# Selective scan in one kernel: GpSimd multiplies a whole step in one instruction, and products and C rows have two places each

## The chip, the cores and the metric

One Trainium2 chip, one of its cores. The metric is the device time of one execution in microseconds. Most repeated executions of a kernel agree within 0.3%.

## The reference, cut to what matters

The kernel computes two layers. The first is attention-like and a mixture of experts, and the change does not touch it. The second is a Mamba block over 4 batches of 2048 tokens, followed by a small mixture of experts on 512 tokens. The part that the change touches is the selective scan, with 512 channels (d) and 16 states (n):

```python
def step(h, ins):
    u_t, dt_t, B_t, C_t = ins
    dA = jnp.exp(dt_t[:, :, None] * A)
    h = dA * h + (dt_t * u_t)[:, :, None] * B_t[:, None, :]
    y_t = jnp.einsum('bdn,bn->bd', h, C_t)
    return (h, y_t)
...
y = y + x_conv * D
y = y * jax.nn.silu(z)
return y @ W_out
```

## The kernel before

Everything is f32. Five engines run their own instruction lists, written out by hand, and meet at counting semaphores (`wait_ge`, `then_inc`); an engine that waits holds everything that stands behind the wait in its list.

For each batch, `projection` makes u, dt, dt*u and the rows of B and C; `selective_scan` runs the recurrence; `output` does the gate, the output product and two layer norms. The first `projection` stands alone, then a loop of three runs scan, output and the next projection in one block, and the last block runs scan and output.

The scan of a batch has 64 steps: 4 quarters (`q`) of 512 tokens (CHUNK), and in each the 16 states (`n`). Channels lie on partitions in 4 groups of 128 (`m`, KI is 4). Step s works like this:

- ScalarE (`scalar`): `decay` makes exp(dt*A) for all four groups, 2048 columns, in `da[s % 2]` (L1600). `save` copies the last column of h to `state` in the first three quarters (L1606). `times_b` multiplies the turned dt*u by B in four instructions (L1593). Once a quarter `keep_y` copies the finished y out of PSUM (L1611), after the last gather of the quarter before; it stands ahead of the `decay` of the quarter's third step.
- TensorE (`tensor`): four `to_channels` of four transposes each bring B*dt*u back to channels in PSUM, one for each group (L1528; called the fills below). Two `gather` of eight transposing matmuls each add the products of h and C into the y banks, for groups 0 and 1 and for groups 2 and 3 (L1547), and the second also adds one skip term (L1553). Its list is: fill of step s+1 for groups 0 and 1, first gather of step s-1, fill of step s+1 for groups 2 and 3, second gather of step s-1. After the last step, `z_proj` of the output stage (L1694) stands behind the gathers of step 62, and the gathers of step 63 stand behind it.
- VectorE (`vector`): four scans of 512 columns (L1655), one for each group, each from `da` and a PSUM bank, into `h[s % 2]`. In the quarters after the first they start from `state`.
- GpSimd (`gpsimd`): two products of 1024 columns, `h` times the C row (L1639), for groups 0 and 1 and for groups 2 and 3. They go round three places: two in `hc` and one in `kept`, a tile that holds the 512 tokens for the last mixture of experts once the scan is over.
- The sync queue (`sync`): the C row of a step comes from DRAM, broadcast to 128 partitions, into one of three places of `c_sb` (L1576), when the product that read that place is done.

h has two places. So the first scan of step s waits for the first product of step s-2, and the third scan for the second product; `hr` counts products, `sd` scans, `yr` gathers.

Of the kernel before, what the change touches and what calls it, by code (L numbers as in the profile page):

```python
# [10 lines left out]
ALU = mybir.AluOpType  # L11
# [3 lines left out]
P = 128  # L15
BATCH, SEQ, D = 4, 2048, 256
TILES = SEQ // P
CHUNK = 512
# [8 lines left out]
KI = INNER // P  # L27
# [986 lines left out]

def layer1(nc, t, out, top, tile, sem, sems, clear, bank, ident, ones, layer_norm, x2_dram, x2T_dram, bc_dram):
    with ExitStack() as L:
        kept = tile(L, "kept", [P, MOE_TOK // P, D])
        with ExitStack() as W:
            w_z = tile(W, "w_z", [P, KC, INNER])
            shared = tile(W, "shared", [P, KI, CHUNK])  # L1020
# [44 lines left out]
            with ExitStack() as s:  # L1065
# [3 lines left out]
                b_cols = tile(s, "b_cols", [P, TILES, STATE])  # L1069
                da = tile(s, "da", [P, 2, KI, CHUNK])  # L1070
                h = tile(s, "h", [P, 2, KI, CHUNK])
                hc = tile(s, "hc", [P, 2, 2, CHUNK])
                c_sb = tile(s, "c_sb", [P, 3, CHUNK])
                state = tile(s, "state", [P, STATE, KI])
                halo = tile(s, "halo", [P, KI, TAPS - 1])
                outside = set(sems)

                def project(g, xT_ready, xT_parts, before=None):
                    return projection(nc, tile, sem, bank, ident, xT, w_x_in, w_dt, w_x, cw, cb, bdt, a_neg, bc_dram, u, dt,
                                      dtu, b_cols, turned0, tok, da, h, hc, c_sb, halo, xT_ready, xT_parts, before)  # L1080

                def scan(g):
                    return selective_scan(nc, sem, bank, ident, tok, u, dt, dtu, b_cols, turned0, skip, a_neg, bc_dram,
                                          kept, da, h, hc, c_sb, state)

                def finish(g, b, ahead, scanned):
                    return output(nc, b, ahead, g, tile, sem, bank, ident, tok, xT, w_z, w_x_in, w_out, t["W_in"], t["W_out"],
# [102 lines left out]


def projection(nc, tile, sem, bank, ident, xT, w_x_in, w_dt, w_x, cw, cb, bdt, a_neg, bc_dram, u, dt, dtu, b_cols,
               turned0, tok, da, h, hc, c_sb, halo, xT_ready, xT_parts, before=None):

    WIDE = TAPS - 1 + HALF
    xin = h[:, :, :, :].rearrange("p a m n -> p (a m n)")[:, 0:3 * WIDE].rearrange("p (w n) -> p w n", w=3)
    slots = da[:, :, :, :].rearrange("p a m n -> p (a m n)")
    xc = slots[:, 0:3 * HALF].rearrange("p (w n) -> p w n", w=3)
    bc = slots[0:2 * STATE, 3 * HALF:4 * HALF]
    th = hc[:, :, :, :].rearrange("p a m n -> p a (m n)")  # L1200
    pr, cp, cv, tr, uu, z = (sem(n) for n in (
        "in_proj", "in_copied", "conv_done", "tanh_ready", "u_ready", "pad_zeroed"))
    bcr, bcc, bt, bk, dr, mn, ln, du, dd, ct = (sem(n) for n in (
# [10 lines left out]
    class Steps:  # L1214
        @staticmethod
        def sync(sp):
            for half in range(2):
                sp.wait_ge(bcc, half + 1)
                sp.dma_start(bc_dram[:, half * HALF:(half + 1) * HALF], bc[:, :]).then_inc(ct, 16)
                if half == 0:  # L1220
                    sp.wait_ge(ct, 16)
                    for n in range(3):
                        sp.dma_start(c_sb[:, n, :], bc_dram[STATE + n, 0:CHUNK].partition_broadcast(P)).then_inc(cl, 16)

        @staticmethod
        def stored(sp):
            sp.wait_ge(ct, 2 * 16)
            sp.wait_ge(cl, 3 * 16)
            if before is not None:
                before.stored(sp)  # L1230

# [233 lines left out]
    return Steps  # L1465


def selective_scan(nc, sem, bank, ident, tok, u, dt, dtu, b_cols, turned0, skip, a_neg, bc_dram, kept, da, h, hc, c_sb,
                   state):

    def turned(q):
# [2 lines left out]
    QUARTERS, N = CHUNKS, STATE  # L1474

    bt_at = [tok[:, 8 * w:8 * w + 8, :].rearrange("p (c i) d -> p c (i d)", c=4) for w in range(2)]
    hc_at = [hc[:, 0, :, :], hc[:, 1, :, :], kept[:, :, :].rearrange("p (m i) d -> p m (i d)", m=2)]

    steps = [(q, n) for q in range(QUARTERS) for n in range(N)]
    S = len(steps)  # L1480

# [1 line left out]
    for s_, (q, n) in enumerate(steps):  # L1483
# [6 lines left out]
    xt, xd, pd, br, dr, sd, sv, hr, yr, yd = (sem(n) for n in (  # L1490
        "dtu_turned", "dtu_kept", "b_times_dtu", "b_ready", "decay_ready", "scan_done", "state_saved", "product",
        "y_added", "y_kept"))
    cl = [sem(f"c_loaded{w}") for w in range(3)]

    def span(q):
        return slice(q * CHUNK, (q + 1) * CHUNK)
# [3 lines left out]

    class Steps:
        all_scanned, y_kept, b_turned = (sd, KI * S), (yd, 4 * QUARTERS), (br, KI * (S - 1))
        y_kept_half, products = (yd, 4 * QUARTERS - 2), (hr, 2 * S)
        @staticmethod
        def tensor(pe, after):
            def place(x):
                kind, i, j = fills[number[x] - 4]
                if kind == "b":
                    pe.wait_ge(sd, KI * i + j + 1)
                else:  # L1510
                    pe.wait_ge(xd, 4 * (i - 1) + j + 1)

            def turn(q, c):
                x = ("turn", q, c)
                place(x)
                for m in range(KI):
                    at = q * CHUNK + c * P
                    op = pe.transpose(fill_bank(x)[:, m * P:(m + 1) * P], dtu[:, m, at:at + P], ident[:, :])
                op.then_inc(xt, 1)

            def to_channels(s_, m):
                x = ("b", s_, m)
                place(x)
                if m == 0:
                    if s_ >= 2:
                        pe.wait_ge(pd, 4 * (s_ - 1))
                for c in range(4):
                    op = pe.transpose(fill_bank(x)[:, c * P:(c + 1) * P], bt_at[s_ % 2][:, c, m * P:(m + 1) * P],  # L1528
                                      ident[:, :])
                op.then_inc(br, 1)  # L1530

            def fill(x):
                kind, i, j = x
                if kind == "b":
                    to_channels(i, j)
                else:
                    turn(i, j)

            def gather(s_, j):
                q, n = steps[s_]  # L1540
                if n == 0 and j == 0 and q:
                    pe.wait_ge(yd, 4 * q)
                pe.wait_ge(hr, 2 * s_ + j + 1)
                for i in range(2):
                    m = 2 * j + i
                    for c in range(4):
                        op = pe.matmul(bank(Y + c)[:, m * P:(m + 1) * P], hc_at[(2 * s_ + j) % 3][:, i, c * P:(c + 1) * P],  # L1547
                                       ident[:, :], start=(n == 0 and m == 0), stop=(n == N - 1),
                                       is_transpose=True, skip_group_check=True)
                if j == 1:  # L1550
                    c, m = n // 4, n % 4
                    at = q * CHUNK + c * P
                    op = pe.matmul(bank(Y + c)[:, m * P:(m + 1) * P], u[:, m, at:at + P], skip[:, m, :],  # L1553
                                   start=False, stop=(n == N - 1), skip_group_check=True)
                op.then_inc(yr, 1)

            done = number["b", 1, 0]
            for s_ in range(S):
                for m in range(KI):
                    while s_ + 1 < S and done <= number["b", s_ + 1, m]:  # L1560
                        fill(fills[done])
                        done += 1
                    if s_ and m % 2:
                        gather(s_ - 1, m // 2)
            after.z_proj(pe, 0)
            gather(S - 1, 0)
            gather(S - 1, 1)
            after.z_proj(pe, 1)

        @staticmethod  # L1570
        def sync(sp):
            for s_, (q, n) in enumerate(steps):
                if s_ < 3:
                    continue
                sp.wait_ge(hr, 2 * (s_ - 3) + 2)
                sp.dma_start(c_sb[:, s_ % 3, :], bc_dram[N + n, span(q)].partition_broadcast(P))\  # L1576
                  .then_inc(cl[s_ % 3], 16)

        @staticmethod
        def scalar(act, after):  # L1580
# [48 lines left out]
        @staticmethod  # L1629
        def gpsimd(pool):  # L1630
            for s_ in range(S):
                if s_ >= 3:
                    pool.wait_ge(cl[s_ % 3], 16 * (s_ // 3))
                for j in range(2):
                    p = 2 * s_ + j
                    pool.wait_ge(sd, KI * s_ + 2 * j + 2)
                    if p >= 3:
                        pool.wait_ge(yr, p - 2)
                    pool.tensor_tensor(hc_at[p % 3], h[:, s_ % 2, 2 * j:2 * j + 2, :],  # L1639
                                       c_sb[:, s_ % 3, :].unsqueeze(1).broadcast_to([P, 2, CHUNK]), ALU.mult)\  # L1640
                        .then_inc(hr, 1)

        @staticmethod
        def vector(dve):
            for s_, (q, n) in enumerate(steps):
                for m in range(KI):
                    if s_:
                        dve.wait_ge(dr, s_)
                        dve.wait_ge(br, KI * (s_ - 1) + m + 1)
                    if m % 2 == 0 and s_ >= 2:  # L1650
                        dve.wait_ge(hr, 2 * (s_ - 2) + m // 2 + 1)
                    if m == 0 and 2 <= s_:
                        dve.wait_ge(sv, min(s_ - 1, (QUARTERS - 1) * N))
                    first = state[:, n, m:m + 1] if q else 0.0
                    dve.tensor_tensor_scan(h[:, s_ % 2, m, :], da[:, s_ % 2, m, :],  # L1655
                                           fill_bank(("b", s_, m)), first, ALU.mult, ALU.add).then_inc(sd, 1)
# [375 lines left out]
```

## Time and profile before

| | us |
|---|---|
| median of 3 runs | 3993.24 |
| lowest and highest run | 3987.85, 3995.3 |
| the profiled execution | 3995.58 |
| its span, first to last instruction | 3993.8 |
| VectorE busy in the span | 2801.4 (70%) |
| GpSimd busy in the span | 1510.7 (38%) |
| mean granted TensorE clock, of full speed | 0.95 |

The span is the profiled execution from its first to its last instruction; 1.8 us of its time lie outside. Times of rows below count from the span's start. A timeline row gives start, length, engine (PE is the matmuls, PEld the weight loads, DVE VectorE, ACT ScalarE, POOL GpSimd), line, operation, output and inputs, count, and in brackets the idle time before it and what ended it. Rows of several instructions in a row are merged: their length runs from the first start to the last end.

### The profile page before, as it was taken

How to read it: one execution, taken by the hardware profiler on the slowest of the kernel's cores; microseconds unless marked ns; L12 is line 12 of the kernel's file. 1: busy time of each engine (PE TensorE's matmuls, PEld its weight loads, DVE VectorE, ACT ScalarE, POOL GpSimd, SP SyncE). 2: the span in 40 equal slices, each digit the busy share in tenths (PEclk: the TensorE clock that was granted, in tenths of full speed). 3: DMA queues.
4: the chain of work that ended last, by engine and by line, in shares of the span. 5: the costliest groups of instructions: out<-in, count | busy, mean ns of one | idle time of the engine just before them, and what ended most of it. 6: DMA issues, size and time to landing. Idle time of an engine off the chain costs nothing. (4 is left out here: it accounts for less than half of the span.)

```text
span 3993.8 us, 53655 instructions
## 1 busy us (share of the span) xinstructions
PE 3410.1 (85%) x19632; PEld 2572.8 (64%) x19632; DVE 2801.4 (70%) x4919; ACT 1955.7 (49%) x3164; POOL 1510.7 (38%) x757
## 2 busy tenths in 40 slices
PE   5898889897999889878888978889888898888879
PEld 2686748783778558663678635777348774488744
DVE  4676457653766467645799766997759987599855
ACT  3222232222223322224799346995459963599700
POOL 1100410031102210030699404995039960199800
PEclk9899989998999989989999999999999999899989
DMA  3000100001000100020111200112101121011220
GB/s 142 1 1 22 65 1 1 22 22 43 1 22 1 64 1 1 22 86 10 36 56 56 74 25 28 57 56 72 36 18 57 56 77 41 10 58 56 68 85 6
DMA packets 103168, 155.31 MB, mean 39 GB/s; under 512 B 15698, under 2 KB 54482, under 8 KB 101346
## 3 DMA queue, kind: packets, MB, share of 16 engines
q1 hardware_dynamic: 102882, 151.62, 11.7%
q8 instruction: 166, 2.72, 0.3%
q14 instruction: 120, 0.98, 0.1%
HBM read 124.81 MB, written 26.78 MB: 38 GB/s over the span
## 5 line engine op out<-in xcount | busy, mean ns | idle before, releaser
L1639 POOL TENSOR_TENSOR hc<-h,c_sb 128x1024 f32<-128x1024 f32 x344 | 810.9, 2382 | 539.7 <-DVE h L1655 532.0
L1655 DVE TENSOR_TENSOR_SCAN h<-da,state,PS 128x512 f32<-128x512 f32 x768 | 902.2, 1257 | 18.2 <-PE PS L1528 12.9
L1528 PE MATMUL PS<-ident,tok 128*128 128x128 f32 x4032 | 599.0, 281 | 144.7 <-DVE h L1655 95.8
L1528 PEld LDWEIGHTS PS<-ident,tok 128*128 128x128 f32 x4032 | 453.7, 142 | 230.1 <-DVE h L1655 169.8
L1600 ACT ACTIVATE da<-dt,a_neg 128x2048 f32<-128x2048 f32 x252 | 505.6, 2006 | 19.9 <-issue 10.2
L1593 ACT ACTIVATE tok<-dtu,b_cols 128x512 f32<-128x512 f32 x768 | 492.2, 724 | 0.0
L109 POOL TENSOR_TENSOR ln_rstd<-ln_var,eps_pow 128x4 f32<-128x4 f32 x65 | 74.3, 1149 | 866.2 <-DVE ln_var L102 866.2
L1639 POOL TENSOR_TENSOR kept<-h,c_sb 128x1024 f32<-128x1024 f32 x168 | 400.5, 2384 | 3.4 <-PE PS L1553 3.4
L727 DVE SCALAR_TENSOR_TENSOR acc<-PS,rw,acc 128x192 f32<-128x192 f32 x768 | 283.0, 413 | 139.1 <-PE PS L645 69.3
L1547 PE MATMUL PS<-ident,hc 128*128 128x128 f32 x2752 | 357.4, 273 | 10.5 <-ACT dtu L1611 7.3
L1547 PEld LDWEIGHTS PS<-ident,hc 128*128 128x128 f32 x2752 | 310.2, 141 | 18.3 <-ACT dtu L1611 9.2
L1655 DVE TENSOR_TENSOR_SCAN h<-da,PS 128x512 f32<-128x512 f32 x256 | 285.5, 1196 | 42.2 <-issue 24.3
L933 POOL TENSOR_TENSOR mix<-attn,rw 128x1024 f32<-128x1024 f32 x64 | 121.4, 1904 | 470.6 <-POOLq L801 420.1
L404 PE MATMUL PS<-xT,wqkvg 128*128 128x512 f32 x512 | 230.5, 612 | 59.9 <-issue 28.5
L1259 PE MATMUL PS<-u,w_dt 128*128 128x512 f32 x512 | 246.9, 639 | 35.8 <-DVE dt L1434 35.8
L645 PE MATMUL PS<-wmoh_hi,xhi 128*128 128x512 f32 x768 | 252.4, 410 | 12.3 <-POOL xlo L609 12.3
L645 PE MATMUL PS<-wmoh_lo,xhi 128*128 128x512 f32 x768 | 246.7, 403 | 0.0
L645 PE MATMUL PS<-wmoh_hi,xlo 128*128 128x512 f32 x768 | 245.1, 400 | 0.0
L609 POOL TENSOR_TENSOR xlo<-xT,xhi 128x256 fp32r<-128x256 f32 x64 | 47.2, 739 | 463.6 <-ACT xhi L751 463.6
L404 PEld LDWEIGHTS PS<-xT,wqkvg 128*128 128x128 f32 x512 | 100.2, 197 | 187.8 <-issue 175.2
L1259 PEld LDWEIGHTS PS<-u,w_dt 128*128 128x128 f32 x512 | 102.6, 204 | 173.6 <-issue 124.9
L901 ACT ACTIVATE prob<-PS,mneg 128x512 f32<-128x512 f32 (+3 forms) x160 | 97.9, 620 | 200.9 <-DVE mneg L869 200.9
(261 smaller groups left out, 6297.1 us busy)
## 6 DMA issues: line engine op xcount, KB each, us to landing
c_sb<-bc_rows SPq DMA_DIRECT2D x256, 256.0 KB, 3.1
xT<-in_xT SPq DMA_DIRECT2D x5, 2048.0 KB, 7.7
tok<-in_x SPq DMA_DIRECT2D x4, 2048.0 KB, 9.1
x_after_layer<-tok SPq DMA_DIRECT2D x16, 512.0 KB, 2.9
xT_after_layer<-x2T_out SPq DMA_DIRECT2D x16, 512.0 KB, 2.7
tok<-x_after_layer SPq DMA_DIRECT2D x16, 512.0 KB, 5.4
out<-tok SPq DMA_DIRECT2D x16, 512.0 KB, 3.0
x2T<-xT_after_layer SPq DMA_DIRECT2D x12, 512.0 KB, 3.6
```

What stands on the lines that cost most here:

```text
L404: last = pe.matmul(bank(4 * (u % 2) + kind), wqkvg[:, k, m * P:(m + 1) * P], xT[:, k, n * CHUNK:(n + 1) * CHUNK], start=(k == 0), stop=(k ...
L645: last = pe.matmul(bank(j), x[:, i % 2, k, :], wmoh[part][:, k, j * CHUNK:(j + 1) * CHUNK], start=(q == 0), stop=(q == len(passes) - 1))
L727: op = dve.scalar_tensor_tensor(acc[:, i % 2, e % 4, :], expert(e), rw[:, i, e:e + 1], acc[:, i % 2, e % 4, :], ALU.mult, ALU.add)
L901: act.activation(prob[:, i % 2, c * CHUNK:c * CHUNK + keys], bank(c)[:, 0:keys], ACT.Exp, bias=mneg[:, i:i + 1], scale=scale, accum_out=de ...
L933: pool.tensor_tensor(mix[:, i % 2, :, :], attn[:, i, :].unsqueeze(1).broadcast_to([P, EXPERTS, EHD]), rw[:, i, :].unsqueeze(2).broadcast_t ...
L1259: last = pe.matmul(bank(where + j)[0:rows, :], weights(k), u[:, k, n * CHUNK:(n + 1) * CHUNK], start=(k == 0), stop=(k == KI - 1))
L1528: op = pe.transpose(fill_bank(x)[:, c * P:(c + 1) * P], bt_at[s_ % 2][:, c, m * P:(m + 1) * P], ident[:, :])
L1547: op = pe.matmul(bank(Y + c)[:, m * P:(m + 1) * P], hc_at[(2 * s_ + j) % 3][:, i, c * P:(c + 1) * P], ident[:, :], start=(n == 0 and m == ...
L1593: act.activation(bt_at[s_ % 2][:, c, :], turned(q)[:, c, :], ACT.Copy, scale=b_cols[:, 4 * q + c, n:n + 1]).then_inc(pd, 1)
L1600: act.activation(da[:, s_ % 2, :, :], dt[:, :, span(q)], ACT.Exp, scale=a_neg[:, n:n + 1]).then_inc(dr, 1)
L1639: pool.tensor_tensor(hc_at[p % 3], h[:, s_ % 2, 2 * j:2 * j + 2, :], c_sb[:, s_ % 3, :].unsqueeze(1).broadcast_to([P, 2, CHUNK]), ALU.mult)\
L1655: dve.tensor_tensor_scan(h[:, s_ % 2, m, :], da[:, s_ % 2, m, :], fill_bank(("b", s_, m)), first, ALU.mult, ALU.add).then_inc(sd, 1)
```

## The change

GpSimd multiplies all four groups of a step in one instruction of 2048 columns, into one of two places of a new tile `products`. Its product waits for all four scans of its step, and `hr` counts one for each step. Both gathers of a step wait for that one product. The first scan of step s waits for the product of step s-2, and the third scan has no wait of its own any more. The C row has two places in place of three, so that its load waits for the product of two steps before. `hc` and the tile of its own for `kept` are gone; `kept` is now half of the second place of `products`. In `projection` the tanh values lie in the first place, and two C rows are loaded ahead in place of three.

```diff
-        kept = tile(L, "kept", [P, MOE_TOK // P, D])
+        products = tile(L, "products", [P, 2, KI, CHUNK])
+        kept = products[:, 1, 0:2, :].rearrange("p m (i d) -> p (m i) d", d=D)
...
-                hc = tile(s, "hc", [P, 2, 2, CHUNK])
-                c_sb = tile(s, "c_sb", [P, 3, CHUNK])
+                c_sb = tile(s, "c_sb", [P, 2, CHUNK])
...
-    th = hc[:, :, :, :].rearrange("p a m n -> p a (m n)")
+    th = products[:, 0, :, :].rearrange("p (w m) n -> p w (m n)", w=2)
...
-                    for n in range(3):
+                    for n in range(2):
                         sp.dma_start(c_sb[:, n, :], bc_dram[STATE + n, 0:CHUNK].partition_broadcast(P)).then_inc(cl, 16)
...
-        y_kept_half, products = (yd, 4 * QUARTERS - 2), (hr, 2 * S)
+        y_kept_half, products = (yd, 4 * QUARTERS - 2), (hr, S)
...
-                pe.wait_ge(hr, 2 * s_ + j + 1)
+                pe.wait_ge(hr, s_ + 1)
...
-                        op = pe.matmul(bank(Y + c)[:, m * P:(m + 1) * P], hc_at[(2 * s_ + j) % 3][:, i, c * P:(c + 1) * P],
+                        op = pe.matmul(bank(Y + c)[:, m * P:(m + 1) * P], products[:, s_ % 2, m, c * P:(c + 1) * P],
...
-                if s_ < 3:
+                if s_ < 2:
                     continue
-                sp.wait_ge(hr, 2 * (s_ - 3) + 2)
-                sp.dma_start(c_sb[:, s_ % 3, :], bc_dram[N + n, span(q)].partition_broadcast(P))\
-                  .then_inc(cl[s_ % 3], 16)
+                sp.wait_ge(hr, s_ - 1)
+                sp.dma_start(c_sb[:, s_ % 2, :], bc_dram[N + n, span(q)].partition_broadcast(P))\
+                  .then_inc(cl[s_ % 2], 16)
...
             for s_ in range(S):
-                if s_ >= 3:
-                    pool.wait_ge(cl[s_ % 3], 16 * (s_ // 3))
-                for j in range(2):
-                    p = 2 * s_ + j
-                    pool.wait_ge(sd, KI * s_ + 2 * j + 2)
-                    if p >= 3:
-                        pool.wait_ge(yr, p - 2)
-                    pool.tensor_tensor(hc_at[p % 3], h[:, s_ % 2, 2 * j:2 * j + 2, :],
-                                       c_sb[:, s_ % 3, :].unsqueeze(1).broadcast_to([P, 2, CHUNK]), ALU.mult)\
-                        .then_inc(hr, 1)
+                if s_ >= 2:
+                    pool.wait_ge(cl[s_ % 2], 16 * (s_ // 2))
+                pool.wait_ge(sd, KI * (s_ + 1))
+                if s_ >= 2:
+                    pool.wait_ge(yr, 2 * (s_ - 1))
+                pool.tensor_tensor(products[:, s_ % 2, :, :], h[:, s_ % 2, :, :],
+                                   c_sb[:, s_ % 2, :].unsqueeze(1).broadcast_to([P, KI, CHUNK]), ALU.mult)\
+                    .then_inc(hr, 1)
...
-                    if m % 2 == 0 and s_ >= 2:
-                        dve.wait_ge(hr, 2 * (s_ - 2) + m // 2 + 1)
+                    if m == 0 and s_ >= 2:
+                        dve.wait_ge(hr, s_ - 1)
```

## Rows read from the trace of the kernel before

**Rows 1.** The page's costliest groups: busy us, mean ns | idle before.

```profile
L1639 POOL TENSOR_TENSOR hc<-h,c_sb 128x1024 f32<-128x1024 f32 x344 | 810.9, 2382 | 539.7 <-DVE h L1655 532.0
L1655 DVE TENSOR_TENSOR_SCAN h<-da,state,PS 128x512 f32<-128x512 f32 x768 | 902.2, 1257 | 18.2 <-PE PS L1528 12.9
...
L1655 DVE TENSOR_TENSOR_SCAN h<-da,PS 128x512 f32<-128x512 f32 x256 | 285.5, 1196 | 42.2 <-issue 24.3
```

**Rows 2.** Busy time in the first and last quarter of the second batch's scan.

```profile
core 0: us, PE busy (x) PEld busy (x) DVE busy (x) ACT busy (x) POOL busy (x), PEclk, DMA share, GB/s
2445.04:2516.41 71.37, 65.20 (x527) 58.98 (x528) 71.33 (x64) 71.23 (x97) 68.96 (x30) 0.95 0.17 53
...
2670.16:2746.47 76.31, 66.13 (x542) 58.88 (x542) 75.17 (x65) 67.47 (x79) 76.30 (x33) 1.00 0.19 62
```

**Rows 3.** Timeline of scans and products, second batch, answers for several short stretches.

```profile
2445.04 4.55 DVE L1655 TENSOR_TENSOR_SCAN h<-da,PS 128x512 f32<-128x512 f32 x4 [12.43 <-issue]
...
2452.85 48.97 DVE L1655 TENSOR_TENSOR_SCAN h<-da,PS 128x512 f32<-128x512 f32 x44
...
2613.90 51.66 DVE L1655 TENSOR_TENSOR_SCAN h<-da,state,PS 128x512 f32<-128x512 f32 x44
...
2732.33 4.77 DVE L1655 TENSOR_TENSOR_SCAN h<-da,state,PS 128x512 f32<-128x512 f32 x4
...
2734.89 2.36 POOL L1639 TENSOR_TENSOR kept<-h,c_sb 128x1024 f32<-128x1024 f32 x1
2737.21 4.71 POOL L1639 TENSOR_TENSOR hc<-h,c_sb 128x1024 f32<-128x1024 f32 x2
```

**Rows 4.** Other GpSimd tensor_tensor groups by shape, whole span.

```profile
L933 POOL TENSOR_TENSOR mix<-attn,rw 128x1024 f32<-128x1024 f32 x64 | 121.4, 1904 | 470.6 <-POOLq L801 420.1 <-PE PS L959 50.3
...
L609 POOL TENSOR_TENSOR xlo<-xT,xhi 128x256 fp32r<-128x256 f32 x64 | 47.2, 739 | 463.6 <-ACT xhi L751 463.6
L393 POOL TENSOR_TENSOR tok<-tok,bout 128x4096 f32<-128x4096 f32 x4 | 35.4, 8849 | 30.2 <-DMA tok<-in_x 30.2
```

**Rows 5.** Timeline around steps 15 to 18, where the first quarter ends.

```profile
2511.94 1.22 DVE L1655 TENSOR_TENSOR_SCAN h<-da,PS 128x512 f32<-128x512 f32 x1
...
2517.44 4.69 POOL L1639 TENSOR_TENSOR hc<-h,c_sb 128x1024 f32<-128x1024 f32 x2
...
2522.18 0.86 PEld L1547 LDWEIGHTS PS<-ident,hc 128*128 128x128 f32 x8 [0.53 <-POOL hc L1639]
...
2527.36 0.22 ACT L1606 ACTIVATE state<-h 128x4 f32<-128x4 f32 x1
...
2527.71 1.28 DVE L1655 TENSOR_TENSOR_SCAN h<-da,state,PS 128x512 f32<-128x512 f32 x1 [1.84 <-PE PS L1528]
```

**Rows 6.** Timeline around steps 31 to 34, where the second quarter ends.

```profile
2588.86 1.25 DVE L1655 TENSOR_TENSOR_SCAN h<-da,state,PS 128x512 f32<-128x512 f32 x1
...
2598.37 0.42 PEld L1528 LDWEIGHTS PS<-ident,tok 128*128 128x128 f32 x4 [0.61 <-DVE h L1655]
...
2598.75 0.91 PEld L1547 LDWEIGHTS PS<-ident,hc 128*128 128x128 f32 x8
...
2599.85 0.47 PEld L1528 LDWEIGHTS PS<-ident,tok 128*128 128x128 f32 x4
...
2604.33 1.28 DVE L1655 TENSOR_TENSOR_SCAN h<-da,state,PS 128x512 f32<-128x512 f32 x1 [1.33 <-PE PS L1528]
```

**Rows 7.** Timeline: first scans of steps 47 and 50.

```profile
2665.48 1.25 DVE L1655 TENSOR_TENSOR_SCAN h<-da,state,PS 128x512 f32<-128x512 f32 x1
...
2680.76 1.28 DVE L1655 TENSOR_TENSOR_SCAN h<-da,state,PS 128x512 f32<-128x512 f32 x1 [1.14 <-ACT da L1600]
```

**Rows 8.** Timeline: first scan of step 63, and the output stage's first weight load.

```profile
2741.70 1.25 DVE L1655 TENSOR_TENSOR_SCAN h<-da,state,PS 128x512 f32<-128x512 f32 x1
...
2746.52 0.30 PEld L1694 LDWEIGHTS PS<-x2T,w_z 128*128 128x128 f32 x2 [1.10 <-DVE h L1655]
```

**Rows 9.** The C row's load in the scan: time from issue to landing.

```profile
DMA to landing us min/median/max: 3.0/3.1/4.0
```

More of the change, by code:

```diff
@@ L1079, in project @@
                     return projection(nc, tile, sem, bank, ident, xT, w_x_in, w_dt, w_x, cw, cb, bdt, a_neg, bc_dram, u, dt,
-                                      dtu, b_cols, turned0, tok, da, h, hc, c_sb, halo, xT_ready, xT_parts, before)
+                                      dtu, b_cols, turned0, tok, da, h, products, c_sb, halo, xT_ready, xT_parts, before)
                 def scan(g):
                     return selective_scan(nc, sem, bank, ident, tok, u, dt, dtu, b_cols, turned0, skip, a_neg, bc_dram,
-                                          kept, da, h, hc, c_sb, state)
+                                          da, h, products, c_sb, state)
                 def finish(g, b, ahead, scanned):
@@ L1192, in projection @@
 def projection(nc, tile, sem, bank, ident, xT, w_x_in, w_dt, w_x, cw, cb, bdt, a_neg, bc_dram, u, dt, dtu, b_cols,
-               turned0, tok, da, h, hc, c_sb, halo, xT_ready, xT_parts, before=None):
+               turned0, tok, da, h, products, c_sb, halo, xT_ready, xT_parts, before=None):
     WIDE = TAPS - 1 + HALF
@@ L1227, in stored @@
             sp.wait_ge(ct, 2 * 16)
-            sp.wait_ge(cl, 3 * 16)
+            sp.wait_ge(cl, 2 * 16)
             if before is not None:
@@ L1465, in projection, with selective_scan @@
     return Steps
-def selective_scan(nc, sem, bank, ident, tok, u, dt, dtu, b_cols, turned0, skip, a_neg, bc_dram, kept, da, h, hc, c_sb,
+def selective_scan(nc, sem, bank, ident, tok, u, dt, dtu, b_cols, turned0, skip, a_neg, bc_dram, da, h, products, c_sb,
                    state):
@@ L1476, in selective_scan @@
     bt_at = [tok[:, 8 * w:8 * w + 8, :].rearrange("p (c i) d -> p c (i d)", c=4) for w in range(2)]
-    hc_at = [hc[:, 0, :, :], hc[:, 1, :, :], kept[:, :, :].rearrange("p (m i) d -> p m (i d)", m=2)]
     steps = [(q, n) for q in range(QUARTERS) for n in range(N)]
@@ L1492, in selective_scan @@
         "y_added", "y_kept"))
-    cl = [sem(f"c_loaded{w}") for w in range(3)]
+    cl = [sem(f"c_loaded{w}") for w in range(2)]
     def span(q):
```

## The prediction

> **What bounds the kernel now.** I read the page's costliest groups first. The two lines of the change, GpSimd's product and VectorE's scan, are its largest users of those engines: 344 products into hc of 2.38 us (the others go into kept), 768 scans of 1.26 us with a state and 256 of 1.20 without [rows 1]. The 1024 scans are four in each of 256 steps, 64 steps in each of four batches. Next I read the busy time of a scan's quarters [rows 2]. VectorE is busy 71.33 of 71.37 us in the first quarter and 75.17 of 76.31 in the last; GpSimd is busy 76.30 of 76.31 there. Two engines are full, so this view doesn't say which one leads.
>
> The timeline does [rows 3]. In the first quarter 44 scans take 48.97 us; without the last scan's own 1.20 that is 47.77 / 43 = 1.111 us from scan to scan, or 4.45 us a step. With a state it is (51.66 - 1.26) / 43 = 1.172, or 4.69 us a step. No gap is left between scans. GpSimd follows: in the step that begins at 2732.33 the second scan ends at about 2734.76 and its product starts at 2734.89; the fourth ends at 2737.10 and its product starts at 2737.21. So VectorE leads by scans that are back to back, and GpSimd answers 0.11 to 0.13 us behind each pair. Its two products (4.71 us for two, 2.33 from start to start) fit the step barely. What keeps VectorE free is that half a step is handed over at a time: the product of groups 0 and 1 is done long before the scan that overwrites them, two steps later.
>
> The exceptions are the ends of the first three quarters. Step 18 starts 15.77 us after step 15 [rows 5], step 34 15.47 us after step 31 [rows 6], step 50 15.28 us after step 47 [rows 7], where three steps alone would be about 14. There ScalarE copies y out after the last gather and only then makes the decay that VectorE waits for.
>
> **The change, part by part.**
>
> *The product.* The trace has none of 2048 columns. A line through 1024 columns (2.383) [rows 1] and 4096 (8.849) [rows 4] gives 2.105 us for 1024 more, so 4.54; a line through 256 (0.739) [rows 4] and 1024 gives 4.57. I take D = 4.55. The bounds are half of the 4096 row, 4.42, and twice the 1024 row, 4.77. GpSimd issues one instruction fewer a step and gains some 0.1 us a step of its own time; since it follows, that alone is worth nothing. The Trainium skill's GPSIMD Engine Reference, section 3.1 (Elementwise), has 4.497 us measured for an f32 tensor_tensor add of 2048 columns; with it the sum below would be 40 us in place of 46.
>
> *The new wait.* This is the main term. A product now starts after all four scans of its step, and the first scan two steps later may not start before it ends, since it overwrites h. Behind this wait VectorE's whole list stands. From the first scan of step s: four scans 4.80 (4.77 in a row [rows 3], and 0.03 more because a scan that had to wait takes 1.28 in place of 1.25 [rows 6]), then 0.13 to GpSimd, then D = 4.55, then back to VectorE. For that last hop no row exists; the nearest is a scan that waited for ScalarE's save, which ended at 2527.58, and began at 2527.71 [rows 5], 0.13, and TensorE's answer to GpSimd, 2522.13 to 2522.18 [rows 5], 0.05. I take 0.10. Two steps cost 4.80 + 0.13 + 4.55 + 0.10 = 9.58 us, where two free ones cost 9.37. In the first quarter the four scans take 4.55 [rows 3], so 9.33 in place of 8.89. Before, this wait was met with about half a step to spare; that spare is what the change uses up.
>
> - First quarter, up to step 15: 7 pairs of 9.33 and one step of 4.48 are 69.79. Before, 2511.94 - 2445.04 = 66.90 [rows 3, 5]. Loss 2.89.
> - Steps 18 to 31: 6 pairs of 9.58 and one step of 4.72 are 62.20; before 2588.86 - 2527.71 = 61.15 [rows 5, 6]. Loss 1.05.
> - Steps 34 to 47: before 2665.48 - 2604.33 = 61.15 [rows 6, 7]. Loss 1.05.
> - Steps 50 to 63: before 2741.70 - 2680.76 = 60.94 [rows 7, 8]. Loss 1.26.
>
> *The gathers.* Both now wait for the whole product, and in TensorE's list the first one stands ahead of two fills and the second gather. In the steady step this is covered: TensorE is busy 66 of 76 us [rows 2], and a fill that comes about 1.3 us after the wait ends is still ahead of the third scan, 2.34 us after it. At a quarter's end nothing covers it. There the product of the last step ends 4.77 + 0.13 + 4.55 = 9.45 us after that step's first scan; then 0.05, the first gather 0.86 [rows 5], one fill 0.43, and from the next fill on the chain is that of before: 2604.33 - 2598.37 = 5.96 us to the scan [rows 6]. Together 16.75 in place of 15.47 for the second quarter, a loss of 1.28, and the same again for the third. For the first quarter, with scans of 4.53, it is 16.51 in place of 15.77, a loss of 0.74.
>
> *The end of a scan.* Before the output stage's first weights (step 63 plus 4.82 us [rows 8]) stand both gathers of step 62. Its product ends 9.48 after its first scan, that is 4.76 after step 63's. Then 0.05, 0.86, and the second gather with the skip term, 2599.85 - 2598.75 = 1.10 [rows 6]: 6.77 in place of 4.82, a loss of 1.95. TensorE leads there, so I pass it on in full.
>
> *C rows.* The load now follows the product of two steps before. That ends 0.10 before the step begins; the load lands 3.1 us later, 4.0 at most in 244 [rows 9]; the product wants it 4.93 after the step begins. Covered by 1 us at least, so nothing. Two C rows instead of three ahead, the tanh values and kept in another place: no instruction grows and nobody waits, nothing.
>
> *Sum.* 2.89 + 0.74 + 1.05 + 1.28 + 1.05 + 1.28 + 1.26 + 1.95 = 11.5 us a batch, 46 us for four. The profiled execution of 3995.58 would become 4041.6. It lies 2.3 above the median of the runs, so the forecast for a median is 3993.2 + 46 = 4039 us.
>
> *Its bounds.* With D = 4.42 and hops of 0.08 and 0.03 a pair costs 9.33 and is free; the first quarter loses 1.1, the quarter ends 0.56, 1.10 and 1.10, the scan's end 1.75: 5.6 a batch, 4016 us. With D = 4.77 and hops of 0.13 both, pairs cost 9.83 and 9.58: 18.5 a batch, 4067 us.
>
> **The rivals.**
>
> *A cheap product (not slower).* The only other 1024-column product on GpSimd, line 933, takes 1.904 us [rows 4]. If the time over that is a cost for each instruction or for the half-step form, the 2048 columns could take 0.23 + 2 x 1.68 = 3.58 us (0.23 is what the line through 1024 and 4096 leaves at zero columns). All pairs are then free, and only the gathers' order costs: 0.31 at two quarter ends and 0.98 at the scan's end, 6 us in all, 3999 us. It decides from a D below about 3.7. Against it: 344 products in this very line took 2.38 [rows 1], their operands keep their form, and 4096 columns without a repeated operand cost 2.16 ns a column. Chance 7%.
>
> *GpSimd's pace sets the step (not slower).* For it speaks GpSimd's 76.30 busy of 76.31 [rows 2]. If so, a step falls from 4.69 to 4.55 in 192 steps, -27 us, while the quarter ends and scan ends still cost 4 x 5.25 = 21: 3987 us. Against it: each product starts only after the scan that it waits for, and the new wait binds anyway once D is over 4.35. Chance 3%.
>
> *The C row is late.* With two places a load longer than about 5 us would hold the product. If each took 0.7 us more than its cover, 0.35 us a step, 64 x 4 steps: +90, 4129 us. Against it: 4.0 is the longest [rows 9]. Chance 4%.
>
> *The shared port.* A longer GpSimd instruction could hold VectorE off for longer. The rows say no: scans and products are busy together for 75.17 and 76.30 of 76.31 us [rows 2], and the first four scans, half of them before any product runs, are as close (4.55 for four) as the 44 behind them [rows 3]. I give it no chance of its own. The Trainium skill, SBUF — State Buffer, section "Who interferes with whom", says that a VectorE instruction with two SBUF inputs and a GpSimd instruction that reads SBUF block each other fully; counting da and state as two inputs, a step would cost 4.69 + 4.55. This trace doesn't agree for the scan, so it must count as one with a single such input.
>
> **How the numbers follow.** The forecast, a stretched step, has 83%; the cheap product 7, GpSimd's pace 3, the late C row 4, and 3 are left for what I don't see. The range reaches a little inside the bounds of D and the hops, 4012 to 4062. 0.2% (8 us) is about what a measurement of this kernel can tell from no change. Faster by that: 3% (a third of GpSimd's pace, most of the unseen). Within it: 9% (the cheap product, the rest of GpSimd's pace). Slower: 88%.
>
> **What would show it.** A product of about 4.55 us; VectorE no longer back to back but with a gap of some 0.2 us before every second step, released by GpSimd; first quarters of 74 to 75 us where they were 71.4; steps 31 to 34 taking 16.7 us; the output stage's first weights some 2 us further behind the last scan. Wrong would be: scans still without gaps (the product is cheap), GpSimd waiting for a DMA before products (the C row), or an output stage that takes the 1.95 us back.

## The result, and the profile after

The changed kernel takes 4051.99 us (median of 4 runs, 4048.0 to 4053.98); the kernel before takes 3990.55 beside it. The ratio is 1.0152, with a 95% interval of 1.0134 to 1.0170: 61 us slower. The forecast was 46 us and 4039 us, in a range of 4012 to 4062. The profiled execution has a span of 4052.2 us, 58.4 more than that of before.

The page's lines that answer to [rows 1] are these; the columns are busy us and mean ns, then idle time before and what ended it.

```profile
L1635 POOL TENSOR_TENSOR products<-h,c_sb 128x2048 f32<-128x2048 f32 x256 | 1167.1, 4562 | 627.7 <-DVE h L1651 616.5
L1651 DVE TENSOR_TENSOR_SCAN h<-da,state,PS 128x512 f32<-128x512 f32 x768 | 912.3, 1259 | 44.6 <-PE PS L1526 19.3
```

The product takes 4.562 us, where two took 2.38 each, or 4.73 us of GpSimd's time, since two in a row overlap a little. So GpSimd is busy for 44 us less than with 810.9 + 400.5 before (the second figure is the page's line of the products into kept). That is the gain, and it does not pay for what comes with it. The scan takes as long as before (1.259 against 1.257), so nothing slows the scan itself. Its idle time grew.

Steps 18 to 20 of the second batch show the wait. These are rows of the timeline.

```profile
2545.43 4.79 DVE L1651 TENSOR_TENSOR_SCAN h<-da,state,PS 128x512 f32<-128x512 f32 x4 [2.33 <-PE PS L1526]
...
2550.36 4.55 POOL L1635 TENSOR_TENSOR products<-h,c_sb 128x2048 f32<-128x2048 f32 x1 [2.56 <-DVE h L1651]
...
2555.11 1.28 DVE L1651 TENSOR_TENSOR_SCAN h<-da,state,PS 128x512 f32<-128x512 f32 x1 [0.20 <-POOL products L1635]
```

The four scans end at 2550.22, the product starts 0.14 later and ends at 2554.91, and the first scan of step 20 starts 0.20 after that. Two steps take 2555.11 - 2545.43 = 9.68 us, where two free ones take 9.37. Before, no scan waited for a product [rows 3].

The first scans of the steps at which the stretches of the forecast begin and end, second batch, and the output stage's first weights:

```profile
2457.87 1.22 DVE L1651 TENSOR_TENSOR_SCAN h<-da,PS 128x512 f32<-128x512 f32 x1 [13.50 <-issue]
...
2528.85 1.22 DVE L1651 TENSOR_TENSOR_SCAN h<-da,PS 128x512 f32<-128x512 f32 x1 [0.33 <-issue]
...
2608.28 1.27 DVE L1651 TENSOR_TENSOR_SCAN h<-da,state,PS 128x512 f32<-128x512 f32 x1
...
2625.09 1.28 DVE L1651 TENSOR_TENSOR_SCAN h<-da,state,PS 128x512 f32<-128x512 f32 x1 [2.34 <-PE PS L1526]
...
2688.04 1.28 DVE L1651 TENSOR_TENSOR_SCAN h<-da,state,PS 128x512 f32<-128x512 f32 x1
...
2704.68 1.28 DVE L1651 TENSOR_TENSOR_SCAN h<-da,state,PS 128x512 f32<-128x512 f32 x1 [2.16 <-ACT da L1598]
...
2767.95 1.28 DVE L1651 TENSOR_TENSOR_SCAN h<-da,state,PS 128x512 f32<-128x512 f32 x1
...
2774.61 0.30 PEld L1690 LDWEIGHTS PS<-x2T,w_z 128*128 128x128 f32 x2
```

The differences of these starts, beside those of [rows 3] and [rows 5 to 8], and the forecast's terms:

| stretch, second batch | before | after | loss | forecast |
|---|---|---|---|---|
| steps 0 to 15 | 66.90 | 70.98 | 4.08 | 2.89 |
| 15 to 18 | 15.77 | 16.58 | 0.81 | 0.74 |
| 18 to 31 | 61.15 | 62.85 | 1.70 | 1.05 |
| 31 to 34 | 15.47 | 16.81 | 1.34 | 1.28 |
| 34 to 47 | 61.15 | 62.95 | 1.80 | 1.05 |
| 47 to 50 | 15.28 | 16.64 | 1.36 | 1.28 |
| 50 to 63 | 60.94 | 63.27 | 2.33 | 1.26 |
| 63 to the output stage's first weights | 4.82 | 6.66 | 1.84 | 1.95 |
| sum | | | 15.26 | 11.50 |

In this batch the terms at the quarter ends and at the scan's end came out within 0.11 us. The terms made of ordinary steps came out too small, each of them.

### The profile page after: what moved, and what is told of

Read it like the earlier page. It is cut to its first block and busy times, and to the rows that moved or that the text cites. A ratio compares the mean times of both kernels' runs of the same rounds, so it can differ in the third digit from the quotient of the medians.

```text
span 4052.2 us, 53147 instructions
## 1 busy us (share of the span) xinstructions
PE 3394.4 (84%) x19632; PEld 2579.1 (64%) x19632; DVE 2816.3 (70%) x4919; ACT 1968.3 (49%) x3164; POOL 1483.2 (37%) x501
## 5 line engine op out<-in xcount | busy, mean ns | idle before, releaser
L1635 POOL TENSOR_TENSOR products<-h,c_sb 128x2048 f32<-128x2048 f32 x256 | 1167.1, 4562 | 627.7 <-DVE h L1651 616.5
L1651 DVE TENSOR_TENSOR_SCAN h<-da,state,PS 128x512 f32<-128x512 f32 x768 | 912.3, 1259 | 44.6 <-PE PS L1526 19.3
L1545 PE MATMUL PS<-ident,products 128*128 128x128 f32 x4096 | 547.7, 277 | 188.9 <-POOL products L1635 173.3
L1545 PEld LDWEIGHTS PS<-ident,products 128*128 128x128 f32 x4096 | 457.1, 142 | 244.5 <-POOL products L1635 224.4
L1526 PE MATMUL PS<-ident,tok 128*128 128x128 f32 x4032 | 546.4, 277 | 53.2 <-DVE h L1651 36.8
L1526 PEld LDWEIGHTS PS<-ident,tok 128*128 128x128 f32 x4032 | 462.7, 143 | 73.5 <-DVE h L1651 49.7
L1259 PE MATMUL PS<-u,w_dt 128*128 128x512 f32 x512 | 237.2, 618 | 35.8 <-DVE dt L1434 35.8
L834 PE MATMUL PS<-v,probT 128*128 128x128 f32 x1088 | 156.2, 284 | 31.5 <-DVE probT L890 31.5
```

The lines of the kernel that those rows point to most:

```text
L834: last = pe.matmul(bank(6 + i % 2)[:, 0:P], probT[:, n % 2, j * P:(j + 1) * P], v[:, a, :], start=(a == 0), stop=(a == i))
L1259: last = pe.matmul(bank(where + j)[0:rows, :], weights(k), u[:, k, n * CHUNK:(n + 1) * CHUNK], start=(k == 0), stop=(k == KI - 1))
L1545: op = pe.matmul(bank(Y + c)[:, m * P:(m + 1) * P], products[:, s_ % 2, m, c * P:(c + 1) * P], ident[:, :], start=(n == 0 and m == 0), sto ...
L1635: pool.tensor_tensor(products[:, s_ % 2, :, :], h[:, s_ % 2, :, :], c_sb[:, s_ % 2, :].unsqueeze(1).broadcast_to([P, KI, CHUNK]), ALU.mult)\
```

## The experiments

The theory after the result: the time is lost because h is handed over by whole steps. VectorE, GpSimd and VectorE again stand in one chain through h, and at the quarter ends TensorE's gathers stand in it too. The rivals: the places (two for products and C rows in place of three, with kept inside), and the size of the instruction itself. Ratios below are to the kernel before, beside each run.

**Halves again, in the new places.**

```diff
...
-                pool.wait_ge(sd, KI * (s_ + 1))
-                if s_ >= 2:
-                    pool.wait_ge(yr, 2 * (s_ - 1))
-                pool.tensor_tensor(products[:, s_ % 2, :, :], h[:, s_ % 2, :, :],
...
+                for j in range(2):
+                    pool.wait_ge(sd, KI * s_ + 2 * j + 2)
+                    if s_ >= 2:
+                        pool.wait_ge(yr, 2 * (s_ - 2) + j + 1)
+                    pool.tensor_tensor(products[:, s_ % 2, 2 * j:2 * j + 2, :], h[:, s_ % 2, 2 * j:2 * j + 2, :],
...
-                    if m == 0 and s_ >= 2:
-                        dve.wait_ge(hr, s_ - 1)
+                    if m % 2 == 0 and s_ >= 2:
+                        dve.wait_ge(hr, 2 * (s_ - 2) + m // 2 + 1)
```

> The changed kernel with two products of 1024 columns a step again, each after its two scans, each handed over by itself to the gathers and to the scans two steps later; products and C rows keep their two places, kept stays inside products. Handing over (my theory): the whole loss goes, 3985 to 3998 us, no gaps before scans. Places (rival: two places for products and C rows, or the new tile, cost the time): it stays at 4040 us or more.

Measured: 3989.26 us beside 3989.46, ratio 1.0004 (0.9994 to 1.0013). The whole loss is gone, and two places, two C rows and the moved kept cost nothing. The group of its scans has the waits of before and none for GpSimd:

```profile
L1652 DVE TENSOR_TENSOR_SCAN h<-da,state,PS 128x512 f32<-128x512 f32 x768 | 902.2, 1258 | 18.2 <-PE PS L1526 12.9 <-ACT da L1598 4.6
```

**Two products, handed over together.** This keeps the hand-over of the change and undoes its single instruction.

```diff
...
-                pool.tensor_tensor(products[:, s_ % 2, :, :], h[:, s_ % 2, :, :],
-                                   c_sb[:, s_ % 2, :].unsqueeze(1).broadcast_to([P, KI, CHUNK]), ALU.mult)\
-                    .then_inc(hr, 1)
+                for j in range(2):
+                    pool.tensor_tensor(products[:, s_ % 2, 2 * j:2 * j + 2, :], h[:, s_ % 2, 2 * j:2 * j + 2, :],
+                                       c_sb[:, s_ % 2, :].unsqueeze(1).broadcast_to([P, 2, CHUNK]), ALU.mult)\
+                        .then_inc(hr, 1)
...
-                        dve.wait_ge(hr, s_ - 1)
+                        dve.wait_ge(hr, 2 * (s_ - 1))
```

> The changed kernel with two products of 1024 columns in a row, both after all four scans, handed over together. Handing over: it is slower than the changed kernel, since two take 4.71 us where the one takes 4.56: 0.15 in 25 pairs of steps, three quarter ends and one scan end a batch, four batches, +17 us on 4052, that is 4062 to 4075. Size (rival: the instruction of 2048 columns is itself the cost, by its length or by the port): it goes back to 3990 to 4005.

Measured: 4065.23 us, ratio 1.0192 (1.0175 to 1.0209), 13 over the changed kernel of the first comparison. So the longer instruction is not the cost; it is a small gain inside the chain that the change itself builds. Together with the run before, this settles it: the same two products cost nothing when each half is handed over, and 76 us when they are handed over together.

**A third place for h.** The third place is w_dt, which the scan doesn't read; each further batch loads it again.

```diff
...
+    h_at = [h[:, 0, :, :], h[:, 1, :, :], third[:, :, :]]
...
-                pool.tensor_tensor(products[:, s_ % 2, :, :], h[:, s_ % 2, :, :],
+                pool.tensor_tensor(products[:, s_ % 2, :, :], h_at[s_ % 3],
...
-                    if m == 0 and s_ >= 2:
-                        dve.wait_ge(hr, s_ - 1)
+                    if m == 0 and s_ >= 3:
+                        dve.wait_ge(hr, s_ - 2)
```

> The changed kernel with a third place for h, so that a scan waits for the product of three steps before; the place is w_dt's, and w_dt is loaded again for each further batch, 1 MB. Handing over: steps are free again and run at 4.45 and 4.69 us; what stays is the quarter ends (0.8 to 2.4, 1.3, 1.3) and the scan's end (1.9), 4 x 6 to 7 us over before: 4010 to 4025. Places: no change, 4045 or more.

Measured: 4017.18 us, ratio 1.0074 (1.0057 to 1.0091): 35 us come back. The timeline of its second batch, steps 16 to 22, has steps of 4.69 and 4.71 us again (2520.02 to 2524.71, 2542.01 to 2546.72), and the gap that stays there is the one at the quarter's end:

```profile
2520.02 4.77 DVE L1654 TENSOR_TENSOR_SCAN h<-da,state,PS 128x512 f32<-128x512 f32 x4
2524.71 4.77 DVE L1654 TENSOR_TENSOR_SCAN w_dt<-da,state,PS 128x512 f32<-128x512 f32 x4
2532.45 9.48 DVE L1654 TENSOR_TENSOR_SCAN h<-da,state,PS 128x512 f32<-128x512 f32 x8 [2.97 <-PE PS L1529]
2542.01 4.79 DVE L1654 TENSOR_TENSOR_SCAN w_dt<-da,state,PS 128x512 f32<-128x512 f32 x4
2546.72 9.46 DVE L1654 TENSOR_TENSOR_SCAN h<-da,state,PS 128x512 f32<-128x512 f32 x8
```

So the two parts of the theory stand apart: the wait through h in ordinary steps, 35 us, and what stays, 28 us over the kernel before beside it. The late gathers make 23 of these: 1.17, 1.32 and 1.32 us at the second batch's quarter ends and 1.89 at its end, times four. The other 6 lie in the first quarters and in three of the last; their cause is open.

**Gathers behind the fills.**

```diff
-                    if s_ and m % 2:
-                        gather(s_ - 1, m // 2)
+                if s_:
+                    gather(s_ - 1, 0)
+                    gather(s_ - 1, 1)
```

> The changed kernel with both gathers of a step behind all four fills of the next in TensorE's list. If the gather ahead of two fills is what lengthens a quarter's end, each of three ends is 0.86 us shorter: 4 x 2.6 = 10 us, 4042. If the quarter ends hang on the product alone: no change, 4050 to 4054.

Measured: 4062.46 us, ratio 1.0185 (1.0168 to 1.0202): 10 us slower, where 10 faster was expected. Two things were wrong in the expectation. First, little was to be had at a quarter's end: the last fill ahead waits for the fourth scan of the next step anyway. In the second batch the three ends took 16.28, 16.68 and 16.50 us in place of 16.58, 16.81 and 16.64. The weight loads there, after step 31's product in the second batch, have the last fill at 2625.29 and the gathers right behind it:

```profile
2625.29 0.42 PEld L1526 LDWEIGHTS PS<-ident,tok 128*128 128x128 f32 x4 [0.75 <-DVE h L1652]
2625.68 1.78 PEld L1545 LDWEIGHTS PS<-ident,products 128*128 128x128 f32 x16
```

Second, some steps got much longer. In four steps of each of the first three quarters a fill waits for ScalarE's copy of the turned dt*u; now both gathers stand behind that fill. After the first quarter's end TensorE stood still there, and came back at half its clock:

```profile
2556.37 0.71 PEld L1526 LDWEIGHTS PS<-ident,tok 128*128 128x128 f32 x4 [2.00 <-ACT dtu L1583]
2557.07 3.43 PEld L1545 LDWEIGHTS PS<-ident,products 128*128 128x128 f32 x16
```

The same 16 weight loads take 3.43 us here and 1.78 above. The granted clock of that stretch, by the view of stretches (the last three columns are the granted clock, the DMA share and GB/s):

```profile
core 0: us, PE busy (x) PEld busy (x) DVE busy (x) ACT busy (x) POOL busy (x), PEclk, DMA share, GB/s
2549.11:2555.73 6.62, 3.27 (x22) 2.12 (x20) 6.62 (x6) 6.62 (x10) 4.33 (x2) 0.98 0.14 46
2555.73:2557.60 1.87, 1.22 (x6) 1.23 (x7) 1.68 (x3) 1.87 (x3) 1.87 (x1) 0.50 0.00 0
2557.60:2560.90 3.30, 3.30 (x17) 3.30 (x16) 1.28 (x1) 3.30 (x7) 0.97 (x1) 0.50 0.21 71
```

0.50 is 1.2 GHz of 2.4. The next step's first scan came after 3.40 us of idle time. The order of the change, with the gathers between the fills, is the better one.

**The wait for the product last.**

```diff
-                    if m == 0 and s_ >= 2:
-                        dve.wait_ge(hr, s_ - 1)
                     if m == 0 and 2 <= s_:
                         dve.wait_ge(sv, min(s_ - 1, (QUARTERS - 1) * N))
+                    if m == 0 and s_ >= 2:
+                        dve.wait_ge(hr, s_ - 1)
```

> The changed kernel with VectorE's wait for the product put behind its wait for the saved state, directly ahead of the scan. From the product's end to the scan the changed kernel's trace shows 0.20 us where the prediction took 0.10. If that is the second wait instruction that VectorE still has to go through, the hop falls by some 0.05 to 0.1 us in 25 pairs a batch: 5 to 10 us, 4042 to 4047. If it is the way from GpSimd to the scan itself: no change, 4050 to 4054.

Measured: 4047.4 us, ratio 1.0144 (1.0124 to 1.0164). The timeline of steps 18 to 20 shows the shorter hop, that is, the time from the product's end to the scan; the product ends at 2549.96 and the scan starts at 2550.09, 0.13 later in place of 0.20:

```profile
2545.40 4.56 POOL L1635 TENSOR_TENSOR products<-h,c_sb 128x2048 f32<-128x2048 f32 x1 [2.71 <-DVE h L1651]
...
2550.09 1.28 DVE L1651 TENSOR_TENSOR_SCAN h<-da,state,PS 128x512 f32<-128x512 f32 x1
```

The time had not settled it, so the changed kernel and this one ran once more beside each other.

> The changed kernel once more, beside the next run on the same chip: 4045 to 4056 us, 1.4 to 1.6% over before.

> VectorE's wait for the product last, once more beside the changed kernel. The trace of the first run shows the hop at 0.11 to 0.12 us in place of 0.20; 25 pairs a batch make 8 to 9 us: 8 us under the changed kernel, with intervals that no longer overlap. If the first run's 5 us were chance: the same time as the changed kernel.

Measured: 4050.3 us, ratio 1.0160 (1.0146 to 1.0174), and 4045.69, ratio 1.0143 (1.0127 to 1.0158). The gain is 5 us in both comparisons, in the expected direction, but the intervals overlap. The traces settle it. Where a scan's last wait was the product, which is some 110 to 120 times in each, the hop is 0.20 us in both traces of the changed kernel and 0.13 in both of this one (not the 0.11 to 0.12 of the expectation). And the scans alone are 10 to 11 us shorter (the table at the end of this section); 0.07 us in 25 pairs of four batches makes 7 of them, and where the rest comes from is not shown.

**The copy of y behind the decay, in the changed kernel and in the kernel before.**

```diff
-                if n == 1 and q:
-                    keep_y(q - 1)
                 if s_ + 1 < S:
                     decay(s_ + 1)
                 if s_:
                     save(s_ - 1)
+                if n == 1 and q:
+                    keep_y(q - 1)
```

> The changed kernel with ScalarE's copy of y behind the decay and the save of the same step, so that a quarter's end no longer holds the decay. The wait through h stays in every pair of steps. If the gather of the last product reaches the scans at a quarter's end only through that copy, three ends a batch fall from 16.6 to about 14.4 us: 4 x 6.7 = 27 us, 4025. If something else holds the scans there too (the fills behind the next gather, which waits for the copy): 4040 or more.

> The kernel before (two products a step, three places) with ScalarE's copy of y behind the decay and the save of the same step. Steps 15 to 18, 31 to 34 and 47 to 50 take 15.8, 15.5 and 15.3 us where three steps alone are 13.7 to 14.1: 4 x 4.7 = 19 us, 3971, if nothing else holds the scans there; 3990 if the gathers behind the copy do.

Measured: the changed kernel falls to 4022.15 us, ratio 1.0079 (1.0059 to 1.0099), some 30 us under the first comparison's median, so the late gather did reach the scans at a quarter's end through this copy. The kernel before falls to 3977.52, ratio 0.9958 (0.9941 to 0.9975): 12 us where 19 were expected, though the interval, 10 to 24 us, allows both. The trace says 12: its scans are 12.1 us shorter, against 26.3 in the changed kernel. So only 14 of those 26 us are a cost of the change, which is what the three quarter ends lost, 4 x (0.81 + 1.34 + 1.36); the rest the kernel before paid as well. Part of the gain, 1.8 us, is held back once a batch: 4 x (4.7 - 1.8) = 11.6. In the second batch step 15 starts at 2510.01 and 14 scans run on without a gap through the quarter's end, but the third scan of step 18 comes 0.89 us late, and the first of step 19 another 0.91:

```profile
2510.01 4.55 DVE L1655 TENSOR_TENSOR_SCAN h<-da,PS 128x512 f32<-128x512 f32 x4
2514.48 11.80 DVE L1655 TENSOR_TENSOR_SCAN h<-da,state,PS 128x512 f32<-128x512 f32 x10
2527.17 2.45 DVE L1655 TENSOR_TENSOR_SCAN h<-da,state,PS 128x512 f32<-128x512 f32 x2 [0.89 <-issue]
```

**Both sides that cost nothing, with the later copy.** The edits of the first experiment and of this last one together.

> Two products of 1024 columns with two full places and two C rows, and the copy of y behind the decay and the save: both sides of the change that cost nothing, with the later copy. 3968 to 3980 us, about 0.4% under before, like the kernel before with the later copy alone; the fourth half place may add 1 to 3 us where the gather behind the copy held the next product.

Measured: 3968.54 us, ratio 0.9956 (0.9942 to 0.9969). This beats both kernels, by 21 us and by 82, with products of half a step, two full places for them and two C rows. It is the copy that gains: the kernel before with the later copy alone has the ratio 0.9958, and its scans are only 1.4 us longer than those here.

**The scans by themselves.** In each trace, the time from a batch's first scan to the output stage's first weights, summed over the four batches:

| run | scans, us | against before |
|---|---|---|
| the kernel before | 1205.90 | |
| the changed kernel, two traces | 1270.08, 1270.28 | +64.2, +64.4 |
| halves again | 1205.92 | 0.0 |
| two products, handed over together | 1284.85 | +79.0 |
| a third place for h | 1234.50 | +28.6 |
| gathers behind the fills | 1283.14 | +77.2 |
| the wait last, two traces | 1260.08, 1259.39 | +54.2, +53.5 |
| the later copy, changed kernel | 1243.80 | +37.9 |
| the later copy, kernel before | 1193.80 | -12.1 |
| halves and the later copy | 1192.43 | -13.5 |

The rest of the execution, which these edits leave alone but for the later loads of w_dt, takes 2774 to 2789 us in these twelve traces. So a whole execution varies by several us for reasons outside the scans, and the scans show the effect of an edit more sharply than the medians.

## Why the prediction was right, point by point

**What bounds the kernel.** Right. VectorE's scans led and GpSimd answered; 44 us less work for GpSimd did not shorten the kernel.

**The product.** 4.55 forecast, 4.562 measured. The line through the rows of 1024 and 4096 columns was the right price; its slope is 2.155 us for 1024 columns, not 2.105, and its 4.54 follows from 2.155. The Trainium skill's 4.497 us (GPSIMD Engine Reference, section 3.1, Elementwise) is 1.4% under the measured time.

**The new wait.** The mechanism was right and one term of it mis-sized: the hop from GpSimd back to VectorE, for which no row existed, was taken as 0.10 us and measured 0.20 (2554.91 to 2555.11). A pair of steps takes 9.68 us, not 9.58. Over 25 pairs a batch and four batches that is 10 us. The measured 0.20 also lies above the hop's own upper bound, 0.13; the range, which allows for a product of up to 4.77 us, held all the same. The experiment with the wait last shows where 0.07 of it lies: VectorE's next wait, for the saved state, stood behind the one for the product, and costs time after the product is done even though it has been met. In the last quarter, where nothing is saved any more and the wait has been met for steps, the hop is the same 0.20.

**The first quarter.** 4.08 lost in the second batch in place of 2.89. The longer hop is 0.7 of the 1.2 missing. Another 0.33 is the gap before step 15, shown above, which ends by nothing that the profile shows (issue); its cause is open. In the third batch the loss was larger, 73.22 us in place of 66.90. TensorE comes out of the pause between batches at a low clock, and this start delayed scans there: the granted clock was 0.62 for the first 14 us, and the timeline of steps 0 to 3 has gaps that TensorE ends:

```profile
2985.90 9.00 DVE L1651 TENSOR_TENSOR_SCAN h<-da,PS 128x512 f32<-128x512 f32 x8 [12.19 <-issue]
2995.27 2.33 DVE L1651 TENSOR_TENSOR_SCAN h<-da,PS 128x512 f32<-128x512 f32 x2 [0.37 <-POOL products L1635]
2998.05 2.33 DVE L1651 TENSOR_TENSOR_SCAN h<-da,PS 128x512 f32<-128x512 f32 x2 [0.45 <-PE PS L1526]
3002.03 4.55 DVE L1651 TENSOR_TENSOR_SCAN h<-da,PS 128x512 f32<-128x512 f32 x4 [1.64 <-PE PS L1526]
```

Before, a batch started at a low clock too, 0.69 in the second batch's first 11.96 us, but VectorE was busy in all of them. No batch of that trace began as low as the third one here, so it is not shown that the half step to spare would have covered this start too.

**The gathers at quarter ends, and the scan's end.** Right in place, and in the second batch in size: 0.81, 1.34 and 1.36 against 0.74, 1.28 and 1.28, and 1.84 against 1.95. The view of ScalarE and TensorE at the second quarter's end shows the chain as forecast: the product ends at 2617.76, the first gather's weights load from 2617.81, two fills and the second gather follow, the copy of y starts at 2620.91, and the scan at 2625.09.

```profile
2613.20 4.56 POOL L1635 TENSOR_TENSOR products<-h,c_sb 128x2048 f32<-128x2048 f32 x1
...
2617.81 0.86 PEld L1545 LDWEIGHTS PS<-ident,products 128*128 128x128 f32 x8 [1.00 <-POOL products L1635]
2618.63 0.90 PEld L1526 LDWEIGHTS PS<-ident,tok 128*128 128x128 f32 x8
2619.51 0.91 PEld L1545 LDWEIGHTS PS<-ident,products 128*128 128x128 f32 x8
...
2620.91 2.07 ACT L1609 ACTIVATE dtu<-PS 128x512 f32<-128x512 f32 x4 [3.23 <-PE PS L1551]
```

What the sum left out is TensorE's clock. TensorE's weight loads now wait for products 216 times, 224 us in all, where they waited 20 times and 9 us before, and some of these waits are followed by half the clock. At the scan's end of the second and of the fourth batch it stood for about the same time behind the product, and the same 16 weight loads followed:

```profile
2772.69 1.73 PEld L1545 LDWEIGHTS PS<-ident,products 128*128 128x128 f32 x16 [2.02 <-POOL products L1635]
...
3829.86 2.71 PEld L1545 LDWEIGHTS PS<-ident,products 128*128 128x128 f32 x16 [2.07 <-POOL products L1635]
```

The granted clock was 1.00 from 2770.00 to 2774.60 and 0.64 from 3829.90 to 3832.00, and the fourth batch's end took 7.92 us in place of 6.66. In the second trace of the changed kernel three of the four ends took 7.7 to 7.9. In the second batch's last quarter, which lost 2.33 us in place of 1.26, the hop is 0.6 of the difference; at step 52 TensorE came back from 1.60 us behind the product at a clock of 0.59, and the third scan came 0.34 late.

**C rows and places.** Right: the run with halves in the new places takes the time of before. In the changed kernel GpSimd's product waited for a C row for 0.3 us in all.

**The sum.** The second batch's 15.3 times four is 61, the difference of the medians, but that is in part chance: the four batches of the trace lost 16.0, 15.3, 17.2 and 15.8 us, 64.2 together. The profiled executions differ by 58.4, because the stages outside the scans took 5.8 us less in the one after. They don't run at the same clock in every execution. The same 25 us of the projection after the first batch, before and after, by the view of stretches:

```profile
2366.00:2391.00 25.00, 19.44 (x38) 8.10 (x37) 16.55 (x15) 15.69 (x15) 0.00 (x0) 0.86 0.00 1
```

```profile
2379.30:2404.30 25.00, 19.43 (x46) 8.21 (x45) 18.25 (x16) 15.69 (x15) 0.00 (x0) 1.00 0.00 1
```

TensorE was granted 0.86 of full speed there before and 1.00 after. What sets that from one execution to the next was not tried, nor whether it makes up the 5.8 us; these stages spread as widely over the traces of the other runs, so the change can't be credited with it.

**The rivals.** The cheap product, GpSimd's pace and the late C row each fell with the rows above. One argument against the cheap product was a misreading: the instruction of 4096 columns does repeat an operand, 256 columns 16 times (L393 of the kernel). The shared port: scans of 1.259 us beside products of 4.562 show no blocking, as the rows of before had it.

## What to carry to other kernels

Here, merging the instructions of an engine that follows saved that engine's time and nothing else; what counted is how soon each part is handed over, and a buffer that was just deep enough for half steps was too shallow for whole ones. Before merging, write down the loop that the buffer closes (fill, hand over, use, hand back) and compare it with as many steps as the buffer has places: here 9.7 us against 9.4. And a step that only copies a result away should stand behind the one that the leading engine waits for.

## What the runs showed of the hardware

A wait that has been met still costs VectorE time when it stands behind the one that is met last: moving the product's wait to the end cut the hop from 0.20 to 0.13 us, each in two traces. With the gathers behind the fills, TensorE's granted clock fell from 0.98 to 0.50 after a stretch in which it was busy for 3.27 of 6.62 us, with a stand of 2.00 us that began near its end, and then 16 weight loads took 3.43 us in place of 1.78. Not every such stand is followed by the lower clock: of two of 2.02 and 2.07 us in the changed kernel only the second was. So a reordering that only makes TensorE wait in another place can cost several us a time: 3.40 us of VectorE's time in the case above.
